# A fused attention stack on one core: the MLP's second projection as three products of split halves, feed-forward weights split early and kept in DRAM

## The chip, the cores and the metric

One core of a Trainium2 chip runs the whole kernel. The metric is device time of one execution, in microseconds (us). TensorE is called PE here, VectorE DVE, ScalarE ACT, GpSimd POOL, and SP is the engine whose queue starts the transfers. All arithmetic results are float32. "f32r" is a float32 number in the reduced form that PE takes in one pass; a product of two plain float32 operands is a pair of records in the profile.

## The reference, cut to what matters

```python
# x: (4, 512, 256)
x = x + attn(layernorm(x))            # 16 heads of 64, causal
x = x + cross_attn(layernorm(x), ctx) # linear attention
h = layernorm(x)
for l in range(2):                    # the feed-forward stack, twice
    q, k, v = split(shift_token(h) @ wqkv[l])     # 256 -> 3 x 512
    h = h + local_attention(rotary(l2norm(q)), rotary(l2norm(k)), v) @ wo[l]
    t = layer_norm(shift_token(h)) @ w1[l] + b1[l]  # 256 -> 2 x 682
    a, g = split(t)
    h = h + (a * gelu(g)) @ w2[l] + b2[l]           # 682 -> 256
x = x + h
```

## The kernel before, in words

Every engine has its own list of work items, written out by hand as strings and expanded by `order_of` (lines 302 to 470): `START_*` for the first units, `UNIT_*` as a repeated pattern, `ENTRY_*` for the passage from the first attention to the feed-forward stack, `STEP_*` repeated for each step, `CLOSE_*` for the end. An engine issues strictly in that order; semaphores hold it until its inputs are there. In a token the number behind "@" says how many units or steps ahead (or, negative, behind) the item's work belongs.

The work has three parts.

1. The first attention: 32 units (4 pairs of heads by 4 batches by 2). A unit projects k and q (`pk`, `pq`) and, for two token tiles, v (`pv`), each as three f32r products of split operands: an operand x is rounded to x_hi by ACT, and x_lo = x - x_hi is made by DVE; the product is hi*lo + lo*hi + hi*hi. Then come scores (`s`), exponentials on ACT (`e`), row sums inverted on DVE (`r`), the scaling of probabilities on POOL (`f`), transposes on PE (`t`) evacuated by DVE and ACT, and weighted values (`z`). A unit takes some 11.7 us. Dummy matmuls (`keep_running`, 24, 14 and 16 of them) stand at the very start in `RUN_IN`, `RUN_MID` and `RUN_MORE`.
2. The entry: output projection (`awo`), cross attention (`kv`, `KV`, `xq`, `xo`, `xw`), the normalizations, and the first items of the feed-forward stack. Here ACT and DVE also split the first layer's wqkv (`weights.0`, lines 1243 to 1249), and DVE multiplies the rotary tables with the scales of both layers (`tab.0`, `tab.1`, lines 1230 to 1240). The first feed-forward tile is `q.0.0`: PE makes q of one token tile, ACT squares it, DVE makes the two rotary products `ra` and `rb` and the norms, POOL adds them and computes the inverse norm, and PE transposes the sum (`Tqk`).
3. The feed-forward stack: 8 steps (2 layers by 4 batches), interleaved so that one step's MLP runs beside the next step's local attention. A step takes some 78 us. Of the MLP, `hnT` transposes the normalized rows (L1792); ACT evacuates the two halves as `hnT` and `hnT_hi` (L958), DVE makes `hnT_lo` (L1303). `hid` 0 to 5 is the first projection as three f32r products; ACT applies gelu (`gates`, L969 and L972), DVE multiplies with the other half into `hid` (L1390). `w20` and `w21` are the second projection, `second_part`: 4 token tiles by 6 hidden tiles in plain float32, lines 1812 to 1823. Once in each layer ACT and DVE split w1 (`wparts`) and wqkv of the next layer (`weights@2`).

The second projection's products come from one line:

```python
ins = product(bank[:, i * D:(i + 1) * D],
              [(hid[0:krows(f), f, t * P:(t + 1) * P], w2[0:krows(f), f, :]) for f in range(NF)])
```

PSUM has eight banks. `t` items (transposes of local probabilities and of `hnT`) take turns in banks 3 and 4; projections take turns in banks 2, 5, 6 and 7. A bank is free again when its reader has counted its `read` semaphore.

The SP queue loads inputs in program order; a wait in it holds all later transfers. In the first attention it waits for each unit's rounded k, and copies its halves to the other partitions (`other_half`).

## Time and profile before

| | us |
|---|---|
| median of 3 runs | 1186.11 (1185.81 to 1186.63) |
| the profiled execution | 1185.69 |
| its span | 1183.9 |
| PE busy | 1148.3 (97%) |
| DVE busy | 817.5 (69%) |
| ACT busy | 692.3 (58%) |
| POOL busy | 567.4 (48%) |

The profiled execution took 1185.69 us from outside, 1.8 more than its span. A span begins with the first instruction and ends with the last one. Matmuls overlap in the array, so what one costs is seen from start to start, and its own duration is longer than that.

### The profile page before, as it was taken

The page shows a single profiled execution, that of the slowest core. Times are in us where ns is not written, and L with a number is a line of the kernel's source. Part 1 is how long each engine was busy: PE and PEld are TensorE (multiplying, and loading weights), DVE is VectorE, ACT ScalarE, POOL GpSimd, SP SyncE. Part 2 cuts the span into 40 slices and gives each one's busy share as a digit, 9 for nine tenths or more (in the row PEclk, how much of TensorE's full clock was granted, in tenths as well). Part 3 has the DMA queues.
Part 4 walks back from the last instruction along what each step waited for, and adds up shares of the span by engine and source line. Part 5 has one row for each costly group of instructions (what it writes and reads, how often), then busy time and mean ns, then how long its engine had stood idle before and what let it go on. Part 6 is the DMA issues. An engine that isn't in the chain of part 4 may idle for free.

```text
span 1183.9 us, 19712 instructions
## 1 busy us (share of the span) xinstructions
PE 1148.3 (97%) x6678; PEld 893.5 (75%) x6678; DVE 817.5 (69%) x2443; ACT 692.3 (58%) x1696; POOL 567.4 (48%) x618
## 2 busy tenths in 40 slices
PE   8999999999999999998989999999999999999998
PEld 6777878778787766776667777777878778777686
DVE  6878778778877456689987567766575775654641
ACT  2678677677777232453676546656465565573831
POOL 2354444544445213148977464655564645561520
PEclk9999999999999999999999999999999999999999
DMA  7213122221212400011030000000001000001000
GB/s 240 54 37 81 37 55 58 60 49 43 55 37 54 160 18 19 1 63 37 3 131 1 1 1 19 1 1 2 1 19 48 27 2 1 1 23 50 19 25 30
DMA packets 30275, 46.15 MB, mean 39 GB/s; under 512 B 4577, under 2 KB 18017, under 8 KB 30177
## 3 DMA queue, kind: packets, MB, share of 16 engines
q1 hardware_dynamic: 30176, 44.90, 13.0%
q8 instruction: 55, 0.90, 0.3%
q14 instruction: 44, 0.35, 0.1%
HBM read 23.92 MB, written 4.19 MB: 24 GB/s over the span
## 4 chain that ended last, share of the span: by engine, by line
PE 87%; DVE 5%; ACT 3%; POOL 3%; issue 2%; DMA 0%; DVEq 0%; ACTq 0%; POOLq 0%
PE psum L1486 53%; PE psum L1587 6%; PE psum L1569 6%; PE psum L1719 5%; PE psum L1768 5%; PE psum L1753 5%; PE psum L1735 4%; PE psum L1701 2%; ACT hnT_hi L958 1%; DVE stats L1030 1%; POOL rn L730 1%; ACT hnT L958 1%; PE psum L1781 1%; DVE xn L1039 0%; PE psum L1675 0%
## 5 line engine op out<-in xcount | busy, mean ns | idle before, releaser
L691 POOL TENSOR_TENSOR probs<-probs,rden 128x128 f32<-128x128 f32 (+3 forms) x256 | 176.5, 721 | 194.6 <-DVE rden L1097 194.6
L928 ACT ACTIVATE lp<-lp,lneg,rn 128x256 f32<-128x256 f32 (+1 forms) x256 | 143.8, 571 | 20.3 <-DVE lneg L1326 20.1
L840 ACT ACTIVATE probs<-probs,negmax 128x128 f32<-128x128 f32 (+3 forms) x256 | 140.7, 551 | 15.8 <-DVE negmax L1092 15.1
L1085 DVE CUSTOM_DVE_ANT_0 probs<-psum,causal 128x512 f32<-128x512 f32 (+3 forms) x256 | 109.9, 485 | 12.7 <-PE psum L1486 12.7
L730 POOL TENSOR_TENSOR rn<-ssm,neg_half 128x8 f32<-128x8 f32 x64 | 106.1, 1658 | 0.0
L1314 DVE CUSTOM_DVE_ANT_0 lp<-psum,local 128x256 f32<-128x256 f32 (+1 forms) x256 | 84.1, 385 | 22.7 <-PE psum L1719 22.6
L721 POOL TENSOR_TENSOR lp<-lp,lrden 128x768 f32<-128x768 f32 x64 | 94.9, 1483 | 0.0
L1486 PE MATMUL psum<-w,hid 124*128 124x256 f32 (+2 forms) x384 | 85.7, 379 | 2.6 <-DVE hid L1390 2.6
L1569 PE MATMUL psum<-ident,probs 128*128 128x128 f32 x640 | 86.0, 273 | 1.5 <-DVE pT L1106 1.1
L1486 PE MATMUL psum<-q,k_rest 128*128 128x256 f32 (+2 forms) x256 | 85.5, 345 | 1.6 <-DVE rowmax L1085 1.6
L1486 PE MATMUL psum<-wqkv_hi,hT_lo 128*128 128x512 f32 x192 | 82.8, 431 | 1.0 <-ACT lv L805 0.9
L718 POOL TENSOR_TENSOR lp<-lp,lrden 128x128 f32<-128x128 f32 x64 | 26.6, 415 | 119.2 <-DVE lrden L1331 119.2
L805 ACT ACTIVATE pT<-psum 128x512 f32<-128x512 f32 (+1 forms) x96 | 47.7, 520 | 59.7 <-PE psum L1569 59.4
L1486 PEld LDWEIGHTS psum<-w,hid 124*128 124x128 f32 (+2 forms) x384 | 72.0, 190 | 13.9 <-issue 4.0
L726 POOL TENSOR_TENSOR ra<-ra,rb 128x512 f32<-128x512 f32 x32 | 41.1, 1284 | 79.6 <-DVE rb L1275 79.6
L915 ACT ACTIVATE sq<-psum 128x512 f32<-128x512 f32 x64 | 38.2, 597 | 69.6 <-PE psum L1486 60.5
L1569 PEld LDWEIGHTS psum<-ident,probs 128*128 128x128 f32 x640 | 73.1, 141 | 7.4 <-POOL probs L691 1.5
L1390 DVE SCALAR_TENSOR_TENSOR hid<-psum,b,gl 124x512 f32<-124x512 f32 (+2 forms) x48 | 36.1, 751 | 60.9 <-PE psum L1486 34.8
L1486 PE MATMUL psum<-q,k 128*128 128x256 f32 (+2 forms) x256 | 77.3, 324 | 0.0
L1587 PE MATMUL psum<-pT,v 128*64 128x256 f32 (+3 forms) x512 | 76.0, 439 | 1.2 <-issue 0.8
L1486 PE MATMUL psum<-wqkv_hi,hT_hi 128*128 128x512 f32 x192 | 76.5, 398 | 0.0
L1486 PE MATMUL psum<-wqkv_lo,hT_hi 128*128 128x512 f32 x192 | 75.9, 395 | 0.0
(171 smaller groups left out, 2999.1 us busy)
## 6 DMA issues: line engine op xcount, KB each, us to landing
k<-k_round SPq DMA_DIRECT2D x128, 128.0 KB, 2.4
x<-in_x SPq DMA_DIRECT2D x8, 512.0 KB, 6.1
aw<-in_w_quads SPq DMA_DIRECT2D x4, 768.0 KB, 5.2
w_raw<-in_w SPq DMA_DIRECT2D x2, 1364.0 KB, 6.4
ctxT<-in_ctxT SPq DMA_DIRECT2D x4, 512.0 KB, 8.5
x_scratch<-x SPq DMA_DIRECT2D x4, 512.0 KB, 3.2
x<-x_scratch SPq DMA_DIRECT2D x4, 512.0 KB, 6.4
wqkv_raw<-in_wqkv SPq DMA_DIRECT2D x1, 1536.0 KB, 11.7
```

The costliest lines, as they stand in the source:

```text
L691: ins = pool.tensor_tensor(pr, pr, rden[:, u % 2, h, i:i + 1].broadcast_to([P, TRI[i]]), ALU.mult)
L721: pool.tensor_tensor(pr, pr, r, ALU.mult).then_inc(l_prob, 1)
L730: pool.tensor_tensor(rn[:, m % 2, t, i, :], ssm[:, i, :], neg_half[:, 0:FH], ALU.pow).then_inc(l_rn, 1)
L840: ins = act.activation(pr, pr, ACT.Exp, bias=negmax[:, u % 2, h, i:i + 1], scale=ADH ** -0.5, accum_out=den[:, u % 2, h, i:i + 1])
L928: ins = act.activation(pr, pr, ACT.Exp, bias=lneg[:, u % 2, h, w:w + 1], scale=rn[:, m % 2, w, 0, 2 * j + h:2 * j + h + 1], accum_out=lden ...
L1085: ins = dve.tensor_tensor_reduce(probs[:, u % 2, h, TRI_AT[i]:TRI_AT[i + 1]], bank[:, at:at + TRI[i]], causal[:, S - TRI[i]:S], 1.0, -3e38 ...
L1314: ins = dve.tensor_tensor_reduce(lp[:, u % 2, h, lo:hi], bank[:, at:at + hi - lo], local[:, LOC - (hi - lo):LOC], 1.0, -3e38, ALU.add, ALU ...
L1486: ins = mm(dst, lhsT, rhs, start=i == 0, stop=i == len(pairs) - 1, **kw)
L1569: ins = pe.transpose(bank[:, at:at + P], probs[:, u % 2, h, lo:lo + P], ident[:, :])
L1587: ins = mm(bank[rows, c * P:S], v[:, b % 2, c, cols], pT[:, h, KEYB_AT[c]:KEYB_AT[c] + KEYB[c]], start=c == 0, stop=c == T - 1)
L1719: ins = mm(pair[h][:, at:at + n].rearrange("p (w k) -> p w k", k=P), lqT[rows, c, d, :], keys[rows], start=True, stop=True)
L1753: ins = mm(bank[rows, c * P:c * P + n], lv[:, m % 2, c, cols], lpT[:, h, c * LOC:c * LOC + n], start=c == 0, stop=c == T - 1, skip_group_c ...
```

## The change

- The product of the second projection becomes three f32r products per tile, of `hid_lo`, `hid_hi` with `w2_lo`, `w2_hi`. ACT rounds each hidden tile (`round_hidden`, items `hs`) and DVE subtracts (`rest_of_hidden`), in place of `hid`.
- All feed-forward weights of both layers (wqkv, w1, w2, wo) are packed by partition in one input, 8360 columns per layer, and cut in 11 parts of 760 columns per layer. In units 4 to 25 of the first attention a part is loaded, rounded by ACT, subtracted by POOL (`part`), and both halves are stored to a DRAM scratch. Later the halves are loaded from there as they are; the splits in the entry and the steps are gone.
- Both layers' rotary tables are made at the end of the first attention, stored to DRAM, and loaded when they are needed into one buffer.
- `hn` now shares memory with `hnT`, so that ACT waits for both transposed halves before it evacuates the first.
- The dummy matmuls at the start are 24 and 18, and v is projected first.
- All orders are written anew.

```diff
-RUN_IN = 24
-RUN_MID = 14
-RUN_MORE = 16
+RUN_FIRST = 24
+RUN_SECOND = 18
...
+W_SIZE = (E2 * INNER,) * 3 + (E2 * 2 * HID, NF * D, FPAIRS * D)
+W_PARTS = 11
+FIRST_PART = 4
+W_PART = W_AT[-1] // W_PARTS
...
-        UNIT_ACT = ("t1 e0@1 pk@2 t3 t5 aw0 pq@2 aw1 e1@1 pv@2 aw2")
-        UNIT_POOL = ("f0@6 f1@6")
+        UNIT_ACT = ("part t1 e0@1 pk@2 t3 t5 aw0 pq@2 aw1 e1@1 pv@2 aw2")
+        UNIT_POOL = ("f0@6 f1@6 part@6")
...
-        STEP_PE = ("v2@1 hnT@-1 q2@1 Ta1 k2@1 Tb1 Sa3 hid0@-1 Tqk1@1 hid1@-1 Sb3 hid2@-1 hid3@-1 q3@1 "
+        STEP_PE = ("q2@1 hnT@-1 v2@1 k2@1 Ta1 Sa3 hid0@-1 Tb1 hid1@-1 Tqk1@1 Sb3 hid2@-1 q3@1 hid3@-1 "
...
+            def load_part(i):
+                l, c = divmod(i, W_PARTS)
+                sp.dma_start(w_raw[:, i % 2, :], a["w_all"][l, :, c * W_PART:(c + 1) * W_PART])\
+                    .then_inc(ld_part[i % 2], 16)
+
+            def store_part(i):
+                l, c = divmod(i, W_PARTS)
+                sp.wait_ge(part_lo, i + 1)
+                for half, tile in enumerate((w_half, w_rest)):
+                    sp.dma_start(w_dram[l, half, :, c * W_PART:(c + 1) * W_PART], tile[:, i % 2, :].bitcast(F32))\
+                        .then_inc(part_st, 16)
...
             for u in range(NU):
                 other_half(u)
                 c, j, b, pair = unit_at(u)
+                i = u - FIRST_PART - 3
+                if 0 <= i < DEPTH * W_PARTS - 2:
+                    sp.wait_ge(part_st, 2 * 16 * (i + 1))
+                    load_part(i + 2)
+                if 0 <= i + 1 < DEPTH * W_PARTS:
+                    store_part(i + 1)
...
+            def rest_of_part(i):
+                pool.wait_ge(part_hi, i + 1)
+                pool.tensor_tensor(w_rest[:, i % 2, :], w_raw[:, i % 2, :], w_half[:, i % 2, :], ALU.subtract)\
+                    .then_inc(part_lo, 1)
...
+            def round_hidden(m, f):
+                rows = FROWS[f]
+                wait_read(act, plan["w1a", m, f])
...
+                copy(hid_hi[0:rows, f, :], hid[0:rows, f, :]).then_inc(hd_hi, 1)
...
+            def rest_of_hidden(m, f):
+                rows = FROWS[f]
+                dve.wait_ge(hd_hi, NF * m + f + 1)
+                dve.tensor_tensor(hid_lo[0:rows, f, :], hid[0:rows, f, :], hid_hi[0:rows, f, :], ALU.subtract)\
+                    .then_inc(hd_lo, 1)
...
             def evac_hnT(m):
...
+                for e in range(E2):
+                    wait_full(act, plan["hnT", m, e])
...
             def second_part(m, tp):
-                for f in range(NF - 3, NF):
-                    wait_read(pe, plan["w1a", m, f])
+                pe.wait_ge(hd_lo, NF * (m + 1))
...
-                                  [(hid[0:krows(f), f, t * P:(t + 1) * P], w2[0:krows(f), f, :]) for f in range(NF)])
+                                  [(h[0:krows(f), f, t * P:(t + 1) * P], w[0:krows(f), f, :]) for f in range(NF)
+                                   for h, w in ((hid_lo, w2_hi), (hid_hi, w2_lo), (hid_hi, w2_hi))])
```

The order on DVE in the entry, before the first rotary tile (`ra<-psum,tab`), was this; `wqkv_lo` is the split of the weights, `tab` the tables:

```order
L1189 TENSOR_TENSOR kvm<-psum,heads 128x128 x4
L1210 TENSOR_SCALAR qss<-qss 128x2
L1214 TENSOR_SCALAR kvs<-kvm,qss 128x128 x2
L1248 TENSOR_TENSOR wqkv_lo<-wqkv_raw,wqkv_hi 128x2x512 x3
L1236 SCALAR_TENSOR_TENSOR tab<-tab,qk_scale 128x256
L1239 SCALAR_TENSOR_TENSOR tab<-tab,qk_scale 128x4x32 x2
L1236 SCALAR_TENSOR_TENSOR tab<-tab,qk_scale 128x256
L1239 SCALAR_TENSOR_TENSOR tab<-tab,qk_scale 128x4x32 x2
L1198 TENSOR_SCALAR qm<-psum,xbq 128x512 x2
L1257 TENSOR_TENSOR hT_lo<-psum,hT_hi 128x512 x2
```

and it is now this, down to the first rotary tile:

```order
L1269 TENSOR_SCALAR qm<-psum,xbq 128x512 x2
L1276 TENSOR_TENSOR qT<-qr,qm 128x512 x2
L1260 TENSOR_TENSOR kvm<-psum,heads 128x128 x4
L1321 TENSOR_TENSOR hT_lo<-psum,hT_hi 128x512 x2
L1269 TENSOR_SCALAR qm<-psum,xbq 128x512 x2
L1281 TENSOR_SCALAR qss<-qss 128x2
L1285 TENSOR_SCALAR kvs<-kvm,qss 128x128 x2
L1335 TENSOR_TENSOR ra<-psum,tab 128x512
L1341 TENSOR_TENSOR rb<-psum,tab 128x512
```

The weights' split and the tables are gone from this place, and the first tile follows at once; the residual additions that stood ahead of it come behind it.

The order on ACT in a step, around the gelu tiles (`gl`), was this; `lp` are the exponentials:

```order
L969 ACT_TABLE_LOAD
L969 ACTIVATE gl<-psum,b 124x512 x4
L805 ACTIVATE lqT<-psum 128x4x128
L915 ACTIVATE sq<-psum 128x512
L928 ACT_TABLE_LOAD
L928 ACTIVATE lp,lden<-lp,lneg,rn 128x128
L928 ACTIVATE lp,lden<-lp,lneg,rn 128x256 x3
L915 ACTIVATE sq<-psum 128x512
L805 ACTIVATE lqT<-psum 128x4x128
L805 ACTIVATE loT<-psum 128x512
L969 ACT_TABLE_LOAD
L969 ACTIVATE gl<-psum,b 122x512
```

and is now this, with the copies that round a hidden tile (`hid_hi<-hid`):

```order
L1030 ACT_TABLE_LOAD
L1030 ACTIVATE gl<-psum,b 124x512
L874 ACTIVATE hid_hi<-hid 124x512
L1030 ACTIVATE gl<-psum,b 124x512
L874 ACTIVATE lqT<-psum 128x512
L1030 ACTIVATE gl<-psum,b 124x512
L874 ACTIVATE hid_hi<-hid 124x512 x2
L980 ACTIVATE sq<-psum 128x512
L1030 ACTIVATE gl<-psum,b 124x512
L980 ACTIVATE sq<-psum 128x512
```

The rounding copies stand right behind the gelus of the tiles they need; the exponentials that stood among the gelus before, each with a table load, are behind the last of them.

## Rows read from the trace of the kernel before

**Rows 1.** The page: each engine's busy time, share of the span, instructions.
```profile
PE 1148.3 (97%) x6678; PEld 893.5 (75%) x6678; DVE 817.5 (69%) x2443; ACT 692.3 (58%) x1696; POOL 567.4 (48%) x618
```

**Rows 2.** Busy time by stretch: PE, PEld, DVE, ACT, POOL, PEclk, DMA share, GB/s.
```profile
200.00:300.00 100.00, 99.41 (x657) 80.31 (x655) 81.21 (x254) 73.19 (x204) 47.71 (x70) 1.00 0.21 52
500.00:540.00 40.00, 36.75 (x168) 26.26 (x166) 35.49 (x83) 21.14 (x38) 20.98 (x22) 1.00 0.14 47
540.00:620.00 80.00, 72.31 (x435) 53.84 (x436) 70.17 (x220) 48.47 (x127) 67.23 (x59) 0.98 0.18 63
700.00:800.00 100.00, 97.53 (x569) 75.90 (x568) 69.31 (x220) 60.64 (x141) 55.30 (x49) 1.00 0.02 6
```

**Rows 3.** Timeline of PE in a unit: start, duration, line, operands.
```profile
210.46 0.28 PE L1486 MATMUL psum<-aw_lo,xnT_hi 128*128 128x256 f32 x1
...
211.75 0.60 PE L1569 MATMUL psum<-ident,probs 128*128 128x128 f32 x4
212.10 0.48 PE L1486 MATMUL psum<-q,k_rest 128*128 128x512 f32 x1
212.42 0.39 PE L1486 MATMUL psum<-q,k 128*128 128x512 f32 x1
212.65 0.34 PE L1486 MATMUL psum<-q,k_rest 128*128 128x384 f32 x1
```

**Rows 4.** Timeline of PE in a step, at the second projection.
```profile
669.58 5.36 PE L1486 MATMUL psum<-w,hid 124*128 124x256 f32 x24
674.77 1.03 PE L1701 MATMUL psum<-ident,ra 128*128 128x128 f32 x8
```

**Rows 5.** Groups by line: the second projection's matmuls and weight loads.
```profile
L1486 PE MATMUL psum<-w,hid 124*128 124x256 f32 (+2 forms) x384 | 85.7, 379 | 2.6 <-DVE hid L1390 2.6
L1486 PEld LDWEIGHTS psum<-w,hid 124*128 124x128 f32 (+2 forms) x384 | 72.0, 190 | 13.9 <-issue 4.0
```

**Rows 6.** Timeline of PE behind hnT, and the wait in PE's list of waits.
```profile
717.16 0.63 PE L1735 MATMUL psum<-ident,lp 128*128 128x128 f32 x4
718.40 0.55 PE L1735 MATMUL psum<-ident,lp 128*128 128x128 f32 x3 [0.61 <-ACT hnT_hi L958]
...
PE psum L1735 <- ACT hnT_hi L958: 5.6, 8, 1.3
```

**Rows 7.** Timeline of DVE and PE in the entry, at the first feed-forward tiles.
```profile
512.24 3.49 DVE L1248 TENSOR_TENSOR wqkv_lo<-wqkv_raw,wqkv_hi 128x1024 fp32r<-128x1024 f32 x3
521.61 0.47 PE L1486 MATMUL psum<-wqkv_hi,hT_lo 128*128 128x512 f32 x1
525.29 0.68 DVE L1269 TENSOR_TENSOR ra<-psum,tab 128x512 f32<-128x512 f32 x1
529.28 0.42 DVE L1236 SCALAR_TENSOR_TENSOR tab<-tab,qk_scale 128x256 f32<-128x256 f32 x1
531.95 0.69 DVE L1269 TENSOR_TENSOR ra<-psum,tab 128x512 f32<-128x512 f32 x1
```

**Rows 8.** Timeline of PE where the next layer's wqkv is split.
```profile
754.50 1.23 PE L1701 MATMUL psum<-ident,ra 128*128 128x128 f32 x8 [1.24 <-DVE hT_lo L1257]
```

**Rows 9.** Timeline of PE at the last step: last hidden tile, then second projection.
```profile
1167.70 0.40 PE L1486 MATMUL psum<-hnT_hi,w_hi 128*128 128x512 f32 x1
1169.93 10.62 PE L1486 MATMUL psum<-w,hid 124*128 124x256 f32 x48 [1.83 <-DVE hid L1390]
```

**Rows 10.** Timeline of DVE at the start.
```profile
17.45 1.39 DVE L1039 TENSOR_SCALAR xn<-x,mv,rstd 128x256 f32<-128x256 f32 x4 [1.32 <-POOL rstd L683]
```

**Rows 11.** Groups by line, kinds of work the change adds or removes.
```profile
L805 ACT ACTIVATE aw_hi<-aw 128x512 fp32r<-128x512 f32 x12 | 7.4, 627 | 5.1 <-DMA aw<-in_w_quads 5.1
L721 POOL TENSOR_TENSOR lp<-lp,lrden 128x768 f32<-128x768 f32 x64 | 94.9, 1483 | 0.0
L1303 DVE TENSOR_TENSOR hnT_lo<-hnT,hnT_hi 128x512 fp32r<-128x512 f32 x16 | 14.0, 883 | 11.7 <-ACT hnT_hi L958 11.7
```

**Rows 12.** Timeline of POOL in a unit of the first attention.
```profile
217.91 2.75 POOL L691 TENSOR_TENSOR probs<-probs,rden 128x128 f32<-128x128 f32 x4 [3.66 <-DVE rden L1097]
```

More of the change, by code:

```diff
@@ L32 @@
 assert FAT[NF] == HID
+W_SIZE = (E2 * INNER,) * 3 + (E2 * 2 * HID, NF * D, FPAIRS * D)
+W_AT = [sum(W_SIZE[:i]) for i in range(len(W_SIZE) + 1)]
+W_PARTS = 11
+FIRST_PART = 4
+W_PART = W_AT[-1] // W_PARTS
+assert W_PART * W_PARTS == W_AT[-1]
 W = 128
@@ L361, in build @@
-        STEP_ACT = ("Tqk0@1 v1@1 AV0 hnT@-1 q2@1 v2@1 Ta1 ea2 Tb1 k2@1 eb2 hid0@-1 hid1@-1 hid2@-1 "
-                    "hid3@-1 Tqk1@1 q3@1 ea3 k3@1 Tqk2@1 AV1 hid4@-1 Ta2 hid5@-1 weights@2 hT@2 eb3 "
-                    "Tqk3@1 q0@2 Tb2 v3@1 k0@2 Ta3 q1@2 AV2 ea0@1 Tb3 k1@2 wparts AV3 Ta0@1 eb0@1 ea1@1 "
-                    "Tb0@1 eb1@1 v0@2")
-        STEP_POOL = ("k3@1 fb2 fa3 fb3 q0@2 k0@2 fa0@1 q1@2 fb0@1 k1@2 norm fa1@1 fb1@1 q2@2 k2@2 fa2@1 "
-                     "q3@2")
-        CLOSE_PE = ("T.29.0 hnT.6 T.29.1 Sa.31 w1.6.0 Sb.31 AV.29 T.30.0 w1.6.1 T.30.1 w1.6.2 AV.30 "
-                    "T.31.0 w1.6.3 w1.6.4 T.31.1 wo_early.7.0 AV.31 wo_early.7.1 wo.7.0 wo.7.1 w1.6.5 "
-                    "sh.7 w2.6.0 hnT.7 w2.6.1 w1.7.0 w1.7.1 w1.7.2 w1.7.3 w1.7.4 w1.7.5 w2.7.0 w2.7.1")
@@ new lines, in build @@
+        STEP_DVE = ("Tqk3 Tb2@-1 Sa0 fb3@-1 q0@1 w20@-2 Sb0 k0@1 Ta3@-1 q1@1 w21@-2 Tb3@-1 fa0 Sa1 k1@1 "
[4 rows of a table added]
+        STEP_ACT = ("Tqk0@1 AV0 q2@1 v1@1 hnT@-1 ea2 k2@1 Ta1 v2@1 eb2 Tb1 hid0@-1 hs0@-1 hid1@-1 Tqk1@1 "
+                    "hid2@-1 hs1@-1 hs2@-1 q3@1 hid3@-1 k3@1 Tqk2@1 hs3@-1 hid4@-1 hid5@-1 hs4@-1 hs5@-1 "
+                    "Ta2 ea3 hT@2 eb3 Tqk3@1 AV1 q0@2 Tb2 v3@1 k0@2 q1@2 Ta3 AV2 ea0@1 Tb3 k1@2 eb0@1 "
+                    "AV3 Ta0@1 ea1@1 Tb0@1 v0@2 eb1@1")
+        STEP_POOL = ("k3@1 fb2 fa3 fb3 q0@2 fa0@1 k0@2 fb0@1 fa1@1 norm fb1@1 q1@2 k1@2 q2@2 k2@2 q3@2 "
+                     "fa2@1")
@@ L402, in step_items @@
                     items.append((what, n))
-                if what == "weights" and n == B:
-                    items.append((what, 1))
-                if what == "tab" and n == B:
-                    items.append((what, 1))
-                if what == "wparts" and n % B == 0:
-                    items.append(("w1_parts", n // B))
             return items
@@ L427, in unit_items @@
                     items.append((what, n, i))
+                if what == "part" and 0 <= n - FIRST_PART < DEPTH * W_PARTS:
+                    items.append((what, n - FIRST_PART))
                 if what == "aw" and j == QUNITS - 3 and c < QUADS - 1:
@@ L607, in _ @@
                 load_x(b)
-            sp.dma_start(wqkv_raw[:, :, :], a["wqkv"][0].rearrange("(k p) c -> p k c", p=P)).then_inc(ld_wqkv, 16)
+            for c in range(3):
+                layer_wqkv_lo(0, c)
             sp.wait_ge(k_both, K_DMAS * NU)
@@ L777, in _ @@
                     probabilities(*at)
+                if what == "part":
+                    rest_of_part(*at)
                 if what == "norm2":
@@ L782, in _ @@
                     query_norms(*at)
-                if what == "weights" and at[0] == 0:
+                if what == "zeros":
                     set_zeros()
@@ L941, in evac_O @@
                 copy(loT[:, FPAIRS - 1 - u % FPAIRS, :], bank[:, :]).then_inc(read[use[0]], 1)
-            def split_w1(l):
-                act.wait_ge(ld_w1, 16 * (l + 1))
-                for e in range(E2):
-                    copy(w1_hi[:, e, :], w1_raw[:, e, :]).then_inc(w1_hi_ok, 1)
             def evac_hnT(m):
@@ L999, in _ @@
                     evac_xo(*at)
-                if what == "weights":
-                    round_weights(*at)
-                if what == "w1_parts":
-                    split_w1(*at)
+                if what == "part":
+                    round_part(*at)
                 if what == "hT":
@@ L1685, in qkv_tile @@
                     if m % B == 0:
-                        pe.wait_ge(w_lo, 3 * l + "qkv".index(what) + 1)
+                        pe.wait_ge(ld_wqkv["qkv".index(what)], 2 * 16 * (l + 1))
                 use = plan[what, m, t]
                 bank = wait_free(pe, use)
-                cols = slice("qkv".index(what) * INNER, ("qkv".index(what) + 1) * INNER)
+                c = "qkv".index(what)
                 rows = slice(t * P, (t + 1) * P)
-                product(bank[:, :], [(h[:, e, rows], w[:, e, cols]) for e in range(E2)
+                product(bank[:, :], [(h[:, e, rows], w[:, c, e, :]) for e in range(E2)
                                      for h, w in ((hT_lo, wqkv_hi), (hT_hi, wqkv_lo), (hT_hi, wqkv_hi))])\
@@ L1913, in by_hidden_tiles, with by_partitions, rows @@
         return tiles
+    def by_partitions(wqkv, w1, w2, wo):
+        def rows(w):
+            w = np.asarray(w)
+            return w.reshape(DEPTH, -1, P, w.shape[-1]).transpose(0, 2, 1, 3).reshape(DEPTH, P, -1)
+        qkv = [rows(np.asarray(wqkv)[..., c * INNER:(c + 1) * INNER]) for c in range(3)]
+        return np.concatenate(qkv + [rows(w1), w2.reshape(DEPTH, P, -1), rows(wo)], -1)
     arrays = {
```

249 lines of the change are left out of this document (140 added, 109 removed), and 95 rows, old and new, of tables (CLOSE_DVE, ENTRY_ACT, ENTRY_DVE, ENTRY_PE).

## The prediction

> **What bounds the kernel now.** Begin with the page's first section: PE is busy 97% of the span, and no other engine is above 69% [rows 1]. A kernel of this kind gets faster by what PE has less to do, or less to wait for; work on the others is free as long as PE finds its inputs. Next read busy time by stretch [rows 2], since the average hides where PE is short. In the first attention PE idles 0.6 us in 100, and in a stretch of steps 2.5 in 100. The entry is different: from 500 to 620 us PE is busy 36.75 + 72.31 = 109.1 us of 120, so it idles 10.9, while DVE is busy 35.49 of 40 and then 70.17 of 80 and POOL 67.23 of 80. The granted clock is 0.98 over the second piece, that is part of it at 1.2 GHz instead of 2.4, which takes up to 0.02 x 80 = 1.6 us more. So two prices rule here: PE's own work everywhere, and the work on DVE in the entry. For PE's work the timeline is read from start to start, because the durations overlap. A lone sign of that: 24 records of the second projection start at 669.58 and the next work at 674.77 [rows 4], 0.216 us each, while each lasts 0.379 [rows 5].
>
> **The product.** The second projection has 8 steps x 4 token tiles x 6 hidden tiles = 192 products, two records each, 384 in all [rows 5]. They take 384 x 0.216 = 82.9 us of PE. The change makes 192 x 3 = 576 f32r matmuls of the same shape, 128 stationary columns and 256 moving ones. Their price is seen in v's projection: eleven of them lie between 210.46 and 211.75 [rows 3] (nine more rows like the first stand between), 0.117 each, with a new stationary operand every time. 576 x 0.117 = 67.4. **Gain 15.5.** The bounds are narrow, 0.115 to 0.120, or 14 to 16.6. That the stationary tile has 124 rows and not 128 should not matter: the plain records of both sizes have one mean.
>
> The Trainium skill ("TensorE: Matmul & The Clock Gate", section "Back-to-back issue gap") gives N/2.4 + 2.5 ns for a matmul of N columns at the full clock, 109 ns at 256. By that the 576 would take 62.8 us and the gain would be 20.1; the 0.117 of this trace is 7% above it, and it decides.
>
> **A change of mode.** The first f32r matmul behind plain ones costs extra: 212.10 to 212.42 is 0.32, the next one of the same size 0.23 [rows 3]. In the new order of a step `w20` stands behind the transposes of `hT`, where before it was plain behind plain; I count one such change more per step. 8 x 0.09 = **0.7 lost**.
>
> **The wait behind hnT.** In each step PE issues the transposes for local head pair a (`Ta1`) soon after `hnT`. They need banks 3 and 4, which ACT holds until it has evacuated `hnT` in four passes. PE gets four of them off at 717.16 and the fifth only at 718.40; at 0.109 each it was due at 717.60, so 0.8 us goes [rows 6]. The list of waits has 8 of this kind, 5.6 us. The new order puts `v2` and `k2` (12 matmuls of 0.23, 2.8 us) between `hnT` and `Ta1` where `q2` alone (1.4 us) stood. ACT's start is later by about 0.45, since it now waits for both halves (four transposes of 0.11), which leaves 1.4 - 0.45 = 0.95 us more cover than before, against a wait of 0.8. `hid0` still has `v2`, `k2`, `Ta1` and `Sa3` ahead of it, so `hnT_lo` is not late. **Gain 5.5**, bounds 0 and 7 x 0.8 + 1.3 = 6.9.
>
> **The split of the next layer's weights** stands ahead of `hT_lo` on DVE once, and PE waits 1.24 us for that [rows 8]. It goes: **gain 1.3**, bounds 0 to 1.4. The loads that take its place start as soon as the old layer's q, k and v are made, and have the whole of two projections and `w20` (some 10 us) as cover for each.
>
> **The entry.** DVE splits the weights from 512.24 to 515.7 (3.5 us), then makes tab.0. PE makes the first q at 521.61; DVE comes to it at 525.29, 3.7 us later. Two tiles on it makes tab.1, from 529.28 to 531.95, 2.7 us [rows 7]. All this is off DVE in the new order, where `q.0.0` also stands ahead of residual work of the cross attention. DVE and POOL form the chain here (POOL needs `ra` and `rb`), so DVE's delay is PE's delay. I take 3.7 + 2.7 = **6.4 gained**. Bounds: 0, if POOL, full from there on, sets the pace anyway; and 10.9 + 1.6 = 12.5, if all idle time and the low clock go with it. The tables are made instead at the end of the first attention, where DVE has 19% to spare [rows 2]; this costs nothing on PE unless inverse sums behind them come late, at most one table's 2.7.
>
> **The start.** 54 dummies become 42, 12 x 0.23 = 2.8 us less of PE, but DVE's chain of statistics and splits holds the first scores. It idles 1.32 us before the second batch's normalization [rows 10], and in the new order it has work there. **Gain 1.3**, bounds 0 and 4.
>
> **What is added beside PE.** Each hidden tile costs ACT a copy (0.63, as the copy of a 128x512 weight) and DVE a subtraction between two SBUF tiles (0.88, as hnT_lo) [rows 11]. That is 6 x 0.63 = 3.8 us of ACT and 5.3 us of DVE in a step of 78; DVE goes from 69% to about 78% there, ACT keeps its share since two of its four table loads in a step are gone by the order. Between the last hidden tile and `w20` PE has `v3` and `hT` (6 x 0.23 + 8 x 0.11 = 2.3 us) and also `AV1` and `Ta2`, 23 matmuls more, which I estimate at 2.5; the chain of gelu and product takes 2.2 from the last matmul's start, as at the end of the kernel [rows 9], and copy and subtraction add 1.5. So 3.7 stands against some 4.8 + 0.2. I cost it at nothing, and each us that DVE is late beyond the 1.3 of slack costs 8 in all. In the first attention a part costs ACT about 0.9 (between the copy of 512 columns and twice it) and POOL 1.48 [rows 11]. It stands behind POOL's second scaling, ahead of an idle time of 3.66 us [rows 12]. SP stores it one unit later, when it is made, so that SP is not held; it has a unit of 11.7 us for three transfers. Nothing.
>
> **The end.** From the start of the last hidden tile's last matmul to the second projection 2.23 us go by [rows 9], with gelu and product in them. Now copy and subtraction follow: 0.63 + 0.7 to 0.88. **1.4 lost.**
>
> **Sum.** -15.5 + 0.7 - 5.5 - 1.3 - 6.4 - 1.3 + 1.4 = -27.9. The profiled execution's 1185.7 gives 1157.8; the median of the runs is 0.4 above it. I say 1158.0. What a measurement of this kernel can tell from no change is about 0.2%, 2.4 us.
>
> **The rivals.** *Only PE's own work counts* (20%): new stalls take the place of the old, in the entry because POOL is full, in the steps because DVE is late with the hidden tiles' rests. For it speaks that each engine's order is new and that DVE was above 85% in the entry. Then -15.5 + 0.7 + 1.4 = -13.4 remains, 1172.3. *More than I count* (15%): the entry loses all its idle time and the start gives 4; -27.9 - 6.1 - 2.7 gives 1149. *Parts on the path* (4%): if ACT's copy delays the exponentials of each unit, 22 x 0.9 = 20 us come back, 1178. Against it is ACT's 73% there.
>
> *Weight loads that don't hide* (3%, the other side). The change turns 384 loads of a stationary operand into 576. One load lasts 0.19 us [rows 5]. If it cannot run wholly beside the matmul before it, the spacing is that of the loads, 0.19: 576 x 0.19 = 109.4 instead of 67.4, 42 us more, 1200. It decides from a spacing of 0.165 on, where the 27.9 are used up. The eleven v products at 0.117 [rows 3] speak against it, their loads being as long.
> The Trainium skill (the same page, "The mechanism") has a rule for this case: a load overlaps matmuls in flight only where its row group differs, and all loads here use all rows. By that rule the change loses; the spacing in this trace does not agree.
>
> A case in which the change isn't what it says is left out: built, it has the 576 matmuls.
>
> **Numbers.** My forecast has 58%. The range that leaves 1 in 10 on each side is 1148.0 to 1172.0: down to the full entry, up to the rival in which only PE's work counts. Chances: faster 0.96, within 0.2% 0.01, slower 0.03.
>
> **What would show it.** Right: 576 matmuls at 0.117; no wait of `Ta1` for `hnT_hi`; DVE at the first `ra` less than 1 us after PE's first q; the clock at 1.0 from 500 to 620; the first attention's units unchanged within 0.1 us. Wrong: PE waiting for `hid_lo` at `w20`, a spacing over 0.125, idle time from 500 to 620 still near 11 us, or PE waiting for transposes' inputs in units 4 to 25.

## The result and the profile after

The changed kernel takes 1179.42 us (median of 5 runs, 1178.17 to 1181.45) beside 1186.37 us before (5 runs, 1185.81 to 1187.03): a ratio of 0.9943, 95% interval 0.9928 to 0.9957. It is faster, as forecast, but by 6.9 us and not by 28; 1179.42 lies outside the range of the prediction. Its profiled execution is the one of 1179.42 us, span 1177.6.

The page's first section, as [rows 1]:
```profile
PE 1134.8 (96%) x6858; PEld 894.6 (76%) x6858; DVE 852.3 (72%) x2481; ACT 707.0 (60%) x1742; POOL 612.8 (52%) x641
```
Busy time by stretch, the columns of [rows 2]:
```profile
200.00:300.00 100.00, 96.36 (x637) 77.65 (x638) 84.79 (x232) 77.56 (x206) 61.21 (x75) 1.00 0.52 150
500.00:540.00 40.00, 39.59 (x183) 29.64 (x182) 29.32 (x66) 19.95 (x38) 16.61 (x20) 1.00 0.25 82
540.00:620.00 80.00, 71.37 (x411) 52.82 (x409) 70.74 (x214) 41.39 (x108) 68.73 (x59) 0.98 0.15 55
700.00:800.00 100.00, 100.00 (x632) 79.39 (x629) 69.81 (x232) 59.03 (x147) 56.24 (x51) 1.00 0.11 38
```
The surprise stands in the first of these rows: PE idles 3.6 us in 100 in the first attention, where it was 0.6 [rows 2], though the matmuls of a unit are the same. The steps (last row) have no idle time left. DVE is busy 70 us in 100 there, where the forecast had some 78.

Laid side by side at the same piece of work (the start of its first matmul in each trace; z is the product of probabilities and v of a unit, xq the cross attention's query projection, wo the local output), the two traces differ so, in us, after minus before:

| stretch | forecast | changed kernel | with POOL's wait | by tile |
|---|---|---|---|---|
| start to z of unit 9 | -1.3 | +1.1 | +0.8 | +0.1 |
| z of unit 9 to z of unit 27 | 0 | +10.2 | 0 | -0.1 |
| on to xq of batch 0 | 0 | +0.8 | +0.8 | +0.7 |
| entry: on to wo of step 0 | -6.4 | -2.7 | -2.7 | -4.4 |
| six steps: on to wo of step 6 | -17.2 | -16.7 | -16.6 | -16.6 |
| close: on to the end | -3.0 | +1.1 | +1.0 | -2.8 |
| sum | -27.9 | -6.3 | -16.8 | -23.1 |

(The forecast of the steps is six products less their mode changes, 6 x 1.85, six hnT waits of 0.8, and the 1.3 of the weights' split; of the close, the rest of those terms plus 1.4. The last two columns are experiments below.) The stretches that missed most: the units by 10.2, the close by 4.1, the entry by 3.7, the start by 2.4.

### The profile page after: what moved, and what is told of

It is laid out like the page before. It is cut to its first block, busy times and chain, and to the rows that moved or that the text cites. A ratio compares the mean times of both kernels' runs of the same rounds, so it can differ in the third digit from the quotient of the medians.

```text
span 1177.6 us, 20315 instructions
## 1 busy us (share of the span) xinstructions
PE 1134.8 (96%) x6858; PEld 894.6 (76%) x6858; DVE 852.3 (72%) x2481; ACT 707.0 (60%) x1742; POOL 612.8 (52%) x641
## 4 chain that ended last, share of the span: by engine, by line
PE 82%; DVE 8%; ACT 5%; issue 2%; DMA 1%; SPq 0%; POOL 0%; DVEq 0%; ACTq 0%; POOLq 0%
PE psum L1551 49%; PE psum L1649 6%; PE psum L1781 5%; PE psum L1830 5%; PE psum L1631 4%; PE psum L1815 4%; PE psum L1797 4%; PE psum L1763 2%; DVE probs L1156 2%; ACT probs L909 2%; DVE negmax L1163 1%; DMA k<-k_round 1%; ACT lp L993 1%; PE psum L1854 1%; PE psum L1737 1%
## 5 line engine op out<-in xcount | busy, mean ns | idle before, releaser
L993 ACT ACTIVATE lp<-lp,lneg,rn 128x256 f32<-128x256 f32 (+1 forms) x256 | 143.6, 568 | 17.3 <-DVE lneg L1385 17.2
L1649 PEld LDWEIGHTS psum<-pT,v 128*64 128x64 f32 x512 | 38.2, 136 | 52.5 <-issue 29.7
L874 ACT ACTIVATE lpT<-psum 128x512 f32<-128x512 f32 x64 | 38.0, 594 | 61.9 <-PE psum L1797 61.6
L1551 PE MATMUL psum<-hnT_lo,w_hi 128*124 128x512 f32 (+2 forms) x176 | 71.8, 408 | 0.8 <-DVE hnT_lo L1362 0.7
L1781 PE MATMUL psum<-lkT,lqT 64*128 64x256 f32 (+1 forms) x512 | 67.4, 382 | 4.0 <-DVE lmax L1373 3.9
```

Of the source, the lines that this page charges most:

```text
L874: return act.activation(dst, src, ACT.Copy)
L993: ins = act.activation(pr, pr, ACT.Exp, bias=lneg[:, u % 2, h, w:w + 1], scale=rn[:, m % 2, w, 0, 2 * j + h:2 * j + h + 1], accum_out=lden ...
L1551: ins = mm(dst, lhsT, rhs, start=i == 0, stop=i == len(pairs) - 1, **kw)
L1649: ins = mm(bank[rows, c * P:S], v[:, b % 2, c, cols], pT[:, h, KEYB_AT[c]:KEYB_AT[c] + KEYB[c]], start=c == 0, stop=c == T - 1)
L1781: ins = mm(pair[h][:, at:at + n].rearrange("p (w k) -> p w k", k=P), lqT[rows, c, d, :], keys[rows], start=True, stop=True)
```

## The experiments

**First round: what holds the units.** In the changed kernel's trace ACT waited for the load of a part (0.75 us in the unit shown below), so the first theory was the load. Four kernels: the load a unit earlier; no parts' work; the plain product; POOL relieved in the entry. Each is the changed kernel with this edit.

```diff
# load early: SP's loop
-                    load_part(i + 2)
                 if 0 <= i + 1 < DEPTH * W_PARTS:
+                    if i >= 0:
+                        sp.wait_ge(part_st, 2 * 16 * (i + 1))
                     store_part(i + 1)
+                if 0 <= i + 1 < DEPTH * W_PARTS - 2:
+                    load_part(i + 3)
```


> The changed kernel, but each part of the weights is loaded one unit earlier: SP stores part i+1 and then loads part i+3, where it loaded part i+2 and then stored i+1. Theory A (the ring of 12.0 us a unit in the first attention closes over the load: key's rounding, SP's four copies of the key, the issue of the load, 3.9 us until it lands, ACT's rounding of the part): ACT no longer waits for w_raw, units 10 to 27 take 11.46 us again, -10 us, 1169 us. Theory B (it is ACT's added copy of 0.84 us that makes exponentials and transposes late): the units stay at 12.0, 1179.4. Theory C (the traffic of loads and stores): also 1179.4.

Measured 1181.38 (1180.55 to 1183.72), ratio to before 0.9954 (0.9939 to 0.9969): no gain. ACT's wait for the part is gone, and most units still take 11.7 to 12.4 us. Theory A is refuted; B and C were left as it seemed. What the trace of this run shows in the unit from 246.84, from DVE, POOL and PE:
```profile
253.62 1.39 DVE L1164 TENSOR_SCALAR negmax<-rowmax 128x4 f32<-128x4 f32 x1
253.16 1.83 POOL L758 TENSOR_TENSOR w_rest<-w_raw,w_half 128x760 fp32r<-128x760 f32 x1
259.00 0.65 PE L1650 MATMUL psum<-pT,v 128*64 128x512 f32 x2 [0.57 <-ACT pT L875]
```
An operation on 4 columns takes 1.39 us, and ends as POOL's subtraction ends (254.99).

```diff
# two parts: order of the parts, SP's loop
-                if what == "part" and 0 <= n - FIRST_PART < DEPTH * W_PARTS:
+                if what == "part" and 0 <= n - FIRST_PART < 2:
...
-                    load_part(i + 2)
...
-                sp.wait_ge(part_lo, i + 1)
+                sp.wait_ge(part_lo, min(i + 1, 2))
```


> The changed kernel, but only the first two of the 22 parts are loaded and split; the other 20 are stored with the halves of these two, so ACT's copies, POOL's subtractions and the loads of 20 parts are gone, and every store is left (the layers' weights are therefore not the reference's). Theory A and theory B: units of 11.46 us, -10 us, 1169 us. Theory C (traffic of the stores): 1179.4. If it comes out below the run with the early load, the difference is what ACT's and POOL's work on the parts costs on the path.

Measured 1167.93 (1165.60 to 1168.67), ratio 0.9834 (0.9817 to 0.9850). Every unit from 5 to 27 is back at its time before, with all stores left: the stores cost nothing. What costs is among the three things that went together, ACT's copies, POOL's subtractions and the loads; the second round tells them apart.

```diff
# plain product: second projection (and no hs on ACT and DVE)
-                  [(h[0:krows(f), f, t * P:(t + 1) * P], w[0:krows(f), f, :]) for f in range(NF)
-                   for h, w in ((hid_lo, w2_hi), (hid_hi, w2_lo), (hid_hi, w2_hi))])
+                  [(hid[0:krows(f), f, t * P:(t + 1) * P], w2[0:krows(f), f, :]) for f in range(NF)])
```


> The changed kernel with the second projection in plain f32 again, two records for each of 192 products, and without the rounding and the rest of the hidden tiles; all else as changed. If the product is worth what its spacing says: 384 x 0.216 = 82.9 against 576 x 0.118 = 68.0, +14.9, less 0.7 for the mode and some 2.7 at the close, where a copy and a subtraction leave the path and the longer product covers the normalization behind it: 1191 us. Rival (the hidden tiles' roundings and rests on ACT and DVE hold PE in the steps, so that part of the gain was given back): clearly less, +6 to +8, 1186. Rival (PE's spacing gains the 20 us of the shorter 109 ns): 1197.

Measured 1189.10, but from 1184.72 to 1192.95 over ten runs, which reaches from below the 1186 of the first rival to above the 1191 of the forecast. Two things spread it. PE's mean granted clock goes from 0.999 in the fastest of the ten to 0.992 in the slowest, and 0.007 of 1185 us is 8.3 us. And the stretch of 18 units is 9.3 us over before in this run's profile, 10.3 in the changed kernel's and 12.9 in that of the next run. So this pair says little about the product; it is repeated below without POOL's subtraction in the way.

```diff
# POOL light: inverse_norms
-   pool.tensor_tensor(rn[...], ssm[:, i, :], neg_half[:, 0:FH], ALU.pow)
+   pool.tensor_tensor(rn[...], ssm[:, i, :], ssm[:, i, :], ALU.subtract)
```


> The changed kernel, but POOL's power of -0.5 for the local heads' norms (17 times 1.68 us between 520 and 620 us) is a subtraction of the sum from itself: the inverse norms are zero, so the local attention is uniform and the output is not the reference's. Theory P (POOL, up to 19.3 us busy of 20 there, sets the pace of the entry): most of the 9 us of PE's idle time between 500 and 620 us and the 0.91 of the clock go, -6 to -9 us, 1171 us. Theory D (DVE, 17 to 19 of 20, with ACT behind it sets the pace): within 1.5 us of the changed kernel, 1178.

Measured 1180.13 (1178.42 to 1182.69). Busy time of this run in the entry:
```profile
540.00:620.00 80.00, 70.92 (x420) 53.31 (x419) 70.81 (x216) 41.61 (x109) 46.82 (x60) 1.00 0.14 49
```
POOL is busy 46.8 us instead of 68.7, and PE idles as before. Theory P is refuted. The entry of this trace is 1.6 us shorter than the changed kernel's, and its clock is 1.00 from 540 to 620 where the changed kernel's is 0.98; the run by tile, with POOL's full work, has the same entry at the same clock (below).

**Second round: POOL waits for DVE.** The first round left one suspect, not foreseen by any theory: negmax. The unit in the changed kernel, from ACT, POOL, DVE, ACT, PE, and the groups of negmax in units 4 to 27 (count: min/median/max ns) of the changed kernel and of the run with two parts:
```profile
253.65 0.84 ACT L874 ACTIVATE w_half<-w_raw 128x760 fp32r<-128x760 f32 x1 [0.75 <-DMA w_raw<-in_w_all]
254.57 1.83 POOL L757 TENSOR_TENSOR w_rest<-w_raw,w_half 128x760 fp32r<-128x760 f32 x1
255.08 1.34 DVE L1163 TENSOR_SCALAR negmax<-rowmax 128x4 f32<-128x4 f32 x1
256.46 0.40 ACT L909 ACTIVATE probs<-probs,negmax 128x128 f32<-128x128 f32 x1 [1.38 <-DVE negmax L1163]
260.42 1.08 PE L1649 MATMUL psum<-pT,v 128*64 128x512 f32 x4 [0.57 <-ACT pT L874]
...
L1163 DVE TENSOR_SCALAR negmax<-rowmax x44: 169/170/1680, 100.5 to 355.5; 128x4 f32<-128x4 f32 x44
```
```profile
L1162 DVE TENSOR_SCALAR negmax<-rowmax x45: 169/171/364, 102.4 to 355.8; 128x4 f32<-128x4 f32 x45
```
So the chain reads: POOL's subtraction starts 0.5 us ahead of negmax; negmax is held until 256.42; four exponentials, the key's rounding and two copies of transposes on ACT stand behind it; z finds them 0.57 us late. The first link, POOL holding DVE, is not a wait on a semaphore: in the list of waits DVE appears only as what ACT waits for. In all, 14 of the 44 negmax here last 0.94 to 1.68 us. Each of them started while a subtraction ran, and ended 0.03 us behind it.

The kernel before has the same sign twice, from DVE and POOL:
```profile
202.97 0.36 DVE L1092 TENSOR_SCALAR negmax<-rowmax 128x4 f32<-128x4 f32 x1
201.49 1.82 POOL L691 TENSOR_TENSOR probs<-probs,rden 128x384 f32<-128x384 f32 x2
```
There negmax falls on the last 0.3 us of POOL's scaling and again ends with it (203.33 and 203.31), where it takes 0.17 otherwise. It could have been read before the change.

The cure keeps all work and only moves POOL's subtraction behind the first negmax of a unit; the second one is 2.9 us later.
```diff
             def rest_of_part(i):
 
                 pool.wait_ge(part_hi, i + 1)
+                pool.wait_ge(s_neg, 2 * (i + FIRST_PART + 1) + 1)
```


> The changed kernel with one wait more: POOL begins the subtraction of a part only when DVE has made the maximum of the next unit's first head (negmax), so the 1.82 us of the subtraction lie between the two small DVE operations negmax (SBUF to SBUF, 4 columns) that stand 2.9 us apart. Every copy, subtraction, load and store is left. Theory E (new: negmax takes 0.17 us alone and up to 1.68 beside POOL's subtraction, since it stands until POOL's instruction is done; the exponentials, the rounding of the key and PE's z are late by that): negmax stays at 0.17, units 10 to 27 take 11.46 us, 1169 us. Theory A (the load of the part closes the ring): the load is as late as before, 1179. Theory B (ACT's copy): 1179 as well.

Measured 1167.81 (1166.96 to 1168.93), ratio 0.9835 (0.9819 to 0.9850), 11.6 us less than the changed kernel. (The two were measured at different times; by their ratios to before it is 1.08%, 12.8 us.) Of this run, DVE and POOL in the same unit, and the group of negmax:
```profile
249.95 0.17 DVE L1164 TENSOR_SCALAR negmax<-rowmax 128x4 f32<-128x4 f32 x1
252.82 0.17 DVE L1164 TENSOR_SCALAR negmax<-rowmax 128x4 f32<-128x4 f32 x1
...
250.26 1.83 POOL L758 TENSOR_TENSOR w_rest<-w_raw,w_half 128x760 fp32r<-128x760 f32 x1 [0.44 <-DVE negmax L1164]
...
L1164 DVE TENSOR_SCALAR negmax<-rowmax x46: 170/170/367, 100.2 to 356.5; 128x4 f32<-128x4 f32 x46
```
The 18 units take 207.2 us as before. Theory E holds in its place, its size and its cure. Theories A, B and C fall with this run, since every load, copy and store is left: they cost nothing there, as forecast. The Trainium skill ("SBUF — State Buffer", section "Who interferes with whom") states the rule: a `tensor_scalar` from SBUF to SBUF can run in a mode that takes a pair of ports shared with GpSimd, and whichever of the two starts first keeps the pair for its whole instruction. The traces agree: negmax takes 0.17 us alone, up to 1.68 beside the subtraction of 1.83, and it ends with it. The rule stood there before the prediction, and I did not weigh it.

The other three of this round stand on the kernel with POOL's wait.
```diff
# q first: ENTRY_ACT, ENTRY_DVE
- xq.3 xo.1 q.0.0 k.0.0
+ xq.3 q.0.0 xo.1 k.0.0
- hT.0 xq.3 kvs.2 q.0.0 k.0.0
+ hT.0 xq.3 q.0.0 kvs.2 k.0.0
```


> The run with POOL's wait, and in the entry ACT squares the first q tile ahead of evacuating the cross attention's output for batch 1, and DVE turns to it ahead of the third batch's kvs: the first product with the cosine comes at about 527 us (on the scale of the changed kernel) instead of 529.7. If DVE's and POOL's chain from the first q tile on sets the pace of the entry: 2 to 2.7 us less than the run with POOL's wait alone, between 1166 and 1167. Rival (the delay is absorbed by a later wait on the chain of the cross attention): no difference, within 0.7 us, 1169.

Measured 1170.87 (1170.07 to 1171.09): 3 us slower. The edit did less than was meant: DVE's first rotary product comes 2.8 us behind PE's first q instead of 3.7, so 1.0 earlier and not 2.7. From PE's first q to wo of step 0 it takes 104.9 us instead of 102.2. The granted clock falls twice in this entry (0.91 from 560 to 580 and 0.91 from 600 to 620) and once with POOL's wait (0.91 from 600 to 620), and one such fall is worth 1.7 us (below). What is left is 0.9 us slower with DVE 1.0 us earlier: PE does not follow DVE's first product, and the premise that DVE's delay there is PE's delay is wrong.

> The run with POOL's wait, with the old kernel's orders of PE, DVE and ACT for the start (units 0 to 3), the dummies as changed (42). The changed kernel reached its tenth unit 1.05 us later than the old one where 1.3 us earlier was forecast. If the new order is to blame (PE stands 3.3 us at 31.6 for a key rest that DVE makes late): 1 to 3.8 us less, about 1167; the fewer dummies then give up to 2.8. If it is the added loads in the start: no gain, 1169.

(The edit replaces the three START orders by the old ones.) Measured 1170.92 (1168.69 to 1174.61): no gain, unit 9 at +1.2 instead of +0.8. PE's stand of 3.1 us is gone, but the clock fell in this run too, earlier (0.83 from 20 to 30). The new order is not to blame.

> The run with POOL's wait, with the second projection in plain f32 and no rounding and rests of the hidden tiles. With the first attention undisturbed in both, the difference is the product alone: 384 x 0.216 = 82.9 against 576 x 0.118 = 68.0 and 0.7 for the mode, 1.4 at the end: +12.8, 1182. If the hidden tiles' rests on DVE (mean 0.84 to 1.31 us, where 0.67 is the least) hold PE in the steps: less, +9 to +10. The earlier pair of profiles, in which the first attention differed, had +5.2.

(The edit of the plain product.) Measured 1176.33 (1175.52 to 1181.59): 8.5 us more than with POOL's wait. From wo of step 1 to wo of step 6 the plain product costs 1.59 us more a step; the product itself, timed from its first matmul to the next work, takes 5.19 us for 24 against 4.31 to 4.40 for 36, or 1.67 a step. The expectation had 12.8. Part of what is missing is the start, which is 2.3 us earlier in this run than with POOL's wait though its code is the same; that is the clock (below). The rests of the hidden tiles do not hold PE in the steps: PE's waits in the trace with POOL's wait name `hid_lo` once, at the end of the kernel.

**Third round: start, entry, close.** Again on the kernel with POOL's wait.
```diff
# start key: START_DVE
- s.0.0 xs.3 s.0.1 xT.2 r.0.0 pk.1 pq.1 r.0.1
+ s.0.0 xs.3 pk.1 s.0.1 pq.1 xT.2 r.0.0 r.0.1
```


> The run with POOL's wait, and in the start DVE makes the rest of unit 1's key ahead of the second head's masked scores of unit 0, and q's behind them, both ahead of the rests of xT for batch 2. There PE stands 3.1 us at 31.6 us until DVE frees the key's bank, and in this run the granted clock is 0.69 in the 10 us behind that stall, where it was 1.00 in the run of the plain product with the same stall. If the stall is DVE's order alone: it shrinks below 1 us, -2 to -2.5, and with the clock at 1.00 another 2.4: 1163 to 1165. Rival (the second head's exponentials are late by the 1.4 us instead and PE stands for them): no gain, 1167 to 1168.

Measured 1174.32 (1171.78 to 1175.04), 6.5 us slower. The rival holds, and costs more than it said: unit 9 is reached 4.3 us later than with POOL's wait alone. PE of this run:
```profile
34.61 0.28 PE L1552 MATMUL psum<-aw_hi,xnT_hi 128*128 128x256 f32 x1
40.87 1.12 PE L1632 MATMUL psum<-ident,probs 128*128 128x128 f32 x4 [5.98 <-POOL probs L751]
```

```diff
# short sums: rotary part on DVE
-  sq[:, i, :].rearrange("p (h d) -> p h d", d=FDH)
+  sq[:, i, :].rearrange("p (h d) -> p h d", d=FDH)[:, :, 0:4]
```


> The run with POOL's wait, but DVE sums the squares of 4 columns of each local head instead of 64: 18 reductions between 520 and 620 us of some 0.2 us instead of 0.67, 8.5 us less on DVE there (norms are then not the reference's). POOL's relief by 26 us gave only 1.6 us in the entry. If DVE's work (17 to 19 us of each 20) sets the pace there: 4 to 8 us less, 1160 to 1164. Rival (the waits are latencies round the ring of PE, ACT, DVE and POOL, no engine's sum): less than 1.5 us, 1166.5.

Measured 1169.14 (1165.12 to 1169.57), not to be told from the kernel with POOL's wait. DVE is busy 59.51 us of 80 in the entry and not 67.44, and PE keeps its longest stalls (2.05 us for lmax, 1.38, 1.27 and 1.15; with POOL's wait 2.11, 1.38, 1.27 and 1.13). The entry of the profile is 1.3 us shorter, with one fall of the clock in either. So neither DVE's sum nor POOL's sets the pace there, and the rival's bound of 1.5 us holds; that the waits are latencies round the ring is what remains, and no run shows it by itself.

```diff
# close: second projection; CLOSE_PE
+  order (i, f) with f = NF - 1 last, pe.wait_ge(hd_lo, NF * (m + 1)) only ahead of it
- w1.6.4 w1.6.5 T.31.1 wo_early.7.0 AV.31 wo_early.7.1 wo.7.0 wo.7.1 sh.7
+ w1.6.4 T.31.1 wo_early.7.0 AV.31 wo_early.7.1 wo.7.0 wo.7.1 w1.6.5 sh.7
```


> The run with POOL's wait, with two edits to the second projection and the close: PE multiplies hidden tiles 0 to 4 of both token tiles before it waits for the rest of tile 5; and the last hidden tile of step 6 stands behind the local output of step 7, where the old order had it. The first covers the last wait of 3.17 us with 30 matmuls of 0.117 (3.5 us): -2.7 to -3.1. The second covers the 0.99 us before the shifted half and part of the 1.93 us before hnT of step 7, against up to 1 us in which the rest of that tile is now late: -1 to -2.5. Together 1162 to 1164. Rival (the chain from the output through statistics and normalization sets the time of the close, whatever PE does in it): only the first counts, 1165.

Measured 1168.94 (1168.18 to 1172.91): no gain. PE now waits 3.20 us at hnT of step 7, behind which the clock is low:
```profile
1128.17 1.62 PE L1855 MATMUL psum<-ident,hn 128*128 128x128 f32 x8 [3.20 <-DVE hn L1432]
```
```profile
1120.00:1140.00 20.00, 16.80 (x105) 15.33 (x104) 10.38 (x23) 5.35 (x8) 8.29 (x5) 0.91 0.23 79
```
The stall before the shifted half is gone, but moved and grown. At the end PE waits 2.4 us, now for tile 4. Two edits and a clock event in one run: what each gave can't be told from it.

**Fourth round: the end, and the clock.**
```diff
# by tile: second_part
-                for i in range(2):
-                    t = 2 * tp + i
-                    ins = product(...)
+                for f, i in [(f, i) for f in range(NF) for i in range(2)]:
+                    t = 2 * tp + i
+                    if i == 0:
+                        pe.wait_ge(hd_lo, NF * m + f + 1)
+                    for n, (h, w) in enumerate(((hid_lo, w2_hi), (hid_hi, w2_lo), (hid_hi, w2_hi))):
+                        ins = mm(bank[:, i * D:(i + 1) * D], ...)
```


> The run with POOL's wait; in the second projection PE takes the hidden tiles one after the other for both token tiles of a bank and waits for each tile's rest by itself (the order of the close as changed). At the end PE has tiles 0 to 3 (24 matmuls of 0.117, 2.8 us) while tile 4's rest is made, which the run with tile 5 alone behind waited 2.52 us for, and tile 5's (3.17 us): the last wait goes below 0.5 us, -2.7 to -3.1, 1164.9. Rival (the wait moves to tile 4 or 5 since DVE makes their rests behind one another): -0.7, 1167.1.

Measured 1164.85 (1162.62 to 1166.25), ratio 0.9814 (0.9798 to 0.9830), 3.0 us less, as expected; all five runs lie below all four with POOL's wait. The end of the changed kernel, then of this run (last matmul of the last hidden tile, first of the second projection):
```profile
1162.01 0.40 PE L1551 MATMUL psum<-hnT_hi,w_hi 128*128 128x512 f32 x1
1165.42 0.39 PE L1551 MATMUL psum<-w_hi,hid_lo 124*128 124x256 f32 x1 [3.01 <-DVE hid_lo L1456]
```
```profile
1148.42 0.40 PE L1552 MATMUL psum<-hnT_hi,w_hi 128*128 128x512 f32 x1
1148.66 0.28 PE L1885 MATMUL psum<-w_hi,hid_lo 124*128 124x256 f32 x1
```
The second projection follows without a wait, 0.24 us instead of 3.41 behind the last hidden tile.

```diff
# dummies: project_v
+                if u == 2:
+                    spare = wait_free(pe, plan["t", 0, 0])
+                    for _ in range(10):
+                        mm(spare[:, :], aw_hi[:, 0, 0, 0:P], xnT_hi[:, 0, 0, :], start=True, stop=True)
```


> The run with POOL's wait and ten dummy matmuls of 512 columns (2.3 us) in the stall of 3.1 to 3.3 us at 31.6. If it is this stall after which the granted clock falls to 0.69 to 0.83 in the 10 us from 30 (in five of eight profiles of these orders, and not in the other three): the clock is 1.00 there in the profile, the tenth unit is reached 1.5 us ahead of the old kernel, and the median loses 1 to 2.4 us, 1165.4 to 1166.8, with a narrower spread. Rival (the clock falls for what PE did before 31 us, or by chance): as before, 1167.8.

(That text miscounts: the clock had fallen there in six of the eight profiles of the first two rounds with these orders, and in eight of eleven up to the run by tile.) Measured 1166.79 (1163.90 to 1170.36), not to be told from 1167.81. The 10 us from 30 with POOL's wait, with the plain product on it, and with the dummies:
```profile
30.00:40.00 10.00, 6.90 (x31) 6.22 (x31) 6.92 (x22) 5.46 (x16) 6.77 (x10) 0.69 0.23 52
```
```profile
30.00:40.00 10.00, 6.90 (x48) 6.07 (x47) 7.89 (x26) 6.31 (x17) 6.78 (x10) 1.00 0.23 52
```
```profile
30.00:40.00 10.00, 9.34 (x57) 7.96 (x56) 7.88 (x26) 6.45 (x17) 6.77 (x10) 1.00 0.23 52
```
The same code with the same stall has a mean clock of 0.69 (a good half of these 10 us at 1.2 GHz) or 1.00. With the dummies it was 1.00 in both profiles; two are too few to call the stall the cause, since it was 1.00 in three of the eleven with the stall and fell in the run with the old orders, which has no such stall. Nor did unit 9 come 1.5 us ahead of the old kernel: it came 0.3 ahead here and 0.7 in the next run. Both have a wait there that no other run has, for the copies of a key:
```profile
84.97 0.47 PE L1552 MATMUL psum<-q,k_rest 128*128 128x512 f32 x1 [0.73 <-DMA k<-k_round]
```

> POOL's wait, the second projection tile by tile, and the dummies: the sum if they are independent, 1162.5 to 1164; if the dummies do nothing, as the run tile by tile, 1165. This is the version meant to beat both kernels.

Measured 1164.31 (1162.65 to 1165.77), ratio 0.9807 (0.9792 to 0.9823). It is 1.9% below before, and its highest run lies 12 us below the changed kernel's lowest. It can't be told from the run by tile alone.

## Why the prediction was right and wrong

The direction was right, the time outside the range. By the prediction's own steps:

- *"Parts in units 4 to 25: nothing"* is the step that failed most: it is 11.6 of the 21.4 us by which the forecast missed. It costed ACT's copy, POOL's subtraction and SP's transfers each against the idle time of its own engine, and for each that was true (the run with POOL's wait has all of them at 1167.8). What it left out is that an instruction on POOL can hold one on DVE without any semaphore between them: negmax, 0.17 us alone, took up to 1.68. The subtraction was also mis-sized, 1.82 us where 1.48 was taken from a product of about as many columns [rows 11]; the idle time of 3.66 us had room for either. The rival that named this place had the wrong engine (ACT's copy), 4% and 1178; its number was near by luck.
- *The product, -15.5 + 0.7*: right in kind. The term was mis-sized in the spacing, 0.120 where 0.117 was taken from v's projection. The mode change came as forecast, 0.08 us once in a step, and brings the mean spacing in `w20` to 0.122. Together 8 x 1.67 = 13.4 gained against 14.8. By the Trainium skill's 109 ns ("TensorE: Matmul & The Clock Gate", section "Back-to-back issue gap") the product alone would have gained 20.1, which the trace does not support. The prediction did not say that the section gives this formula for a matmul by itself, and that in a stream it lets the weight loads set the spacing as well. The rival of weight loads that don't hide is refuted: a load lasts 0.19, and of the 576 matmuls all but the first ones of a group follow in some 0.12. The end of a projection in the changed kernel:
```profile
682.43 0.28 PE L1551 MATMUL psum<-w_hi,hid_lo 128*128 128x256 f32 x1
682.54 0.28 PE L1551 MATMUL psum<-w_lo,hid_hi 128*128 128x256 f32 x1
682.66 0.28 PE L1551 MATMUL psum<-w_hi,hid_hi 128*128 128x256 f32 x1
682.78 0.92 PE L1763 MATMUL psum<-ident,ra 128*128 128x128 f32 x7
```
- *The wait behind hnT, -5.5, and the split of the next layer's weights, -1.3*: right. Neither wait is in PE's list any more, and the six steps give 16.7 against 17.2.
- *The entry, -6.4*: 2.7. The step that failed is "DVE's delay is PE's delay". The splits and tables did leave DVE, but its first rotary product is still 3.7 us behind PE's first q (526.00), as it was before [rows 7], and not less than 1 us as forecast; now it is ACT's squares that it waits for last:
```profile
529.73 0.69 DVE L1335 TENSOR_TENSOR ra<-psum,tab 128x512 f32<-128x512 f32 x1 [0.88 <-ACT sq L980]
```
  Having it 1.0 us earlier gave PE nothing, relieving POOL by 22 us gave nothing, and relieving DVE by 8 us gave 1.3 us at most. The clock moves this stretch by 1.7 us: the same orders give -2.7 where it is 0.91 from 600 to 620 and -4.4 where it is 1.00. That does not excuse the forecast, since the kernel before has such a fall in its entry as well (0.91 from 540 to 560): with one fall in each, the orders gave 2.7. PE's stalls of over 0.3 us in the entry sum to 10.8 us before and 8.2 with POOL's wait. Which chain sets the rest stays open. With POOL's wait, then by tile:
```profile
600.00:620.00 20.00, 18.35 (x114) 12.84 (x114) 15.20 (x55) 11.74 (x35) 15.02 (x13) 0.91 0.67 253
```
```profile
600.00:620.00 20.00, 18.58 (x121) 13.82 (x122) 16.04 (x59) 12.51 (x38) 14.67 (x13) 1.00 0.67 253
```
- *The start, -1.3*: +1.1, and this is the clock (0.71 from 30 to 40, 1.00 before). In the run of the plain product on POOL's wait, where it stayed at 1.00, unit 9 came 1.5 us earlier than before, as forecast. The forecast took the clock to be the same in both kernels.
- *The end, +1.4*: the chain was right (3.2 instead of 2.0 us of standing, +1.2), but the close as a whole gave +1.1 where -3.0 was forecast. I priced the last step and not the order of the close, which the change also rewrites: PE now stands 0.8 us before the shifted half (before, the last hidden tile's matmuls lay there), 1.8 at hnT of step 7 and 0.6 behind it, since the new product is shorter and covers less of the normalization. A product that is shortened takes cover from what runs beside it.
```profile
1140.83 1.09 PE L1854 MATMUL psum<-ident,hn 128*128 128x128 f32 x8 [1.77 <-DVE hn L1431]
```
  The cover is seen in the run of the plain product on POOL's wait: with the longer product PE waits 0.86 us there and not 1.77. About 1 us more is the new order by itself: the first run of the plain product has the old product in the new order and one fall of the clock in its close, as before, and from wo of step 6 to the end it takes 99.90 us where the kernel before takes 98.95. Whether another order would give that back was not shown; the one run that tried was spoilt by the clock.

Had the parts cost nothing in the units, the result would have been that of POOL's wait, 1167.8: inside the range, 10 us above the forecast.

## What to carry to other kernels

Work that fits in an engine's idle time is not free yet: where POOL and DVE both read SBUF, look at which DVE instructions run beside the added POOL instruction, and let POOL wait for the small ones on the critical path; a `negmax` of 4 columns that lasts 1.3 us and ends with POOL's instruction is the sign, and it may already stand in the trace before the change. Before a difference of 1 to 2 us is put down to an edit, compare the granted clock of the same stretch in both traces. Where the last wait of a kernel is for the last of several operands, let PE take the others first and wait for each by itself. When a matmul group gets shorter, list what it covered.
